# Second layer's attention: VectorE instead of ScalarE copies the mask of each odd key tile's second score bank into PSUM

## The chip, the cores and the metric

The kernel runs on one core of a Trainium2 chip. The metric is the device time of one execution in microseconds (us). TensorE does the matrix products, ScalarE (ACT) and VectorE (DVE) the elementwise work, GpSimd (POOL) some more of it, and SyncE (SP) issues DMA transfers. PSUM is the memory of eight banks that TensorE writes its products to; a bank holds 512 fp32 values in each of 128 partitions.

## What is computed

A small network of six blocks runs over x, 2 sequences of 256 rows with 256 features. Two of the blocks are cross attentions over a context of 4096 keys for each sequence. The change concerns the second one:

```
Q = query @ Wq.T + bq;  K = key @ Wk.T + bk;  V = value @ Wv.T + bv      # 16 heads of 16 features
energy = einsum('bhqd,bhkd->bhqk', Q, K) / sqrt(16)
energy = where(mask == 0, -1e20, energy)                                   # mask: 256 queries x 4096 keys
attention = softmax(energy, axis=-1)
x = x + einsum('bhqk,bhkd->bhqd', attention, V) ... @ Wo.T + bo
```

The first cross attention is the same without the mask, with a relative position bias. Between them lie a state-space block and a gated feed-forward block, behind them a time-mixing block and a quantized feed-forward block.

## The kernel before

**Steps.** Both attentions are done in 8 steps (g, b): g is one of 4 groups of four heads, b one of 2 sequences. The order is (0,0), (0,1), (1,0), ..., (3,1). A step goes twice over its keys.

**Units: the row maxima.** In the first pass there are 64 units (4 heads x 2 tiles of 128 queries x 8 chunks of 512 keys). TensorE multiplies (L477) into one of three PSUM banks, in turn; VectorE reads the bank, adds the mask and takes the maximum (L582, in the first attention L579 without mask). The semaphore at_seen counts read units, and TensorE writes unit u only when unit u - 3 has been read. When all 64 are read, VectorE makes the negated maxima of the step and splits them in three bf16 parts: five small instructions, L593 to L601, called the maxima below (`at_dve_top`). TensorE transposes these (L497, called rows) into one of the same three banks, and ScalarE writes them as three more rows of the queries (L609, two instructions). With them the scores come out with the maximum already subtracted.

**Score tiles: softmax and values.** In the second pass there are 32 key tiles i of 128 keys. Tile i uses PSUM banks 0 and 1 if i is even, 2 and 3 if it is odd, two heads to a bank. The first bank's mask is put there by a matmul with the identity (L511). The second bank's mask is copied there by ScalarE (L632) right after its exp of tile i - 2 (L628) has freed the banks, and TensorE waits for that copy (semaphore at_masked) before it adds the third and fourth head's scores (L520). Tiles 0 and 1 of a step have both masks from matmuls. After exp, TensorE multiplies with the values (L539) into bank 6, and ScalarE saves that bank at the end of a step (L617).

**How the passes mix.** TensorE's order is written out in `at_pe_step`: while it does the score tiles of step `cur` it does the units of step `nxt`. In pair j of key tiles (j = 0 to 15) it does scores 2j + 2, half of the pair's units, scores 2j + 3, the other half, then the values of tiles 2j and 2j + 1. PER_PAIR gives the units of each pair: 5, then 4 eleven times, 5, 2, 4, 4. From pair 13 on (OWN) the units are the first ten (LEAD) of the step `after` the next. So units 0 and 1 of that step come with scores 28 and 29, units 2 to 5 with scores 30 and 31, and then the rows of `nxt`; pair 15 does scores 0 and 1 of `nxt` with units 6 to 9. Each engine's queue is served strictly in the order written.

**Loops.** TensorE's loop runs over g for 3 passes of two steps, and group 3 is written out behind it. ScalarE's loop has 3 passes between written-out ends. VectorE's loop of the second attention (L699) has 4 passes of two steps, 406 instructions to a pass; in the first attention the step (0,1) stands ahead of the loop, and the loop has 3 passes.

Of the kernel before, what the change touches and what calls it, by code (L numbers as in the profile page):

```python
# [14 lines left out]
B, T, D = 2, 256, 256  # L15
# [8 lines left out]
NG = H // HG  # L24
NT = S // 128
# [18 lines left out]
PER_PAIR = (5, 4, 4, 4, 4, 4, 4, 4, 4, 4, 4, 4, 5, 2, 4, 4)  # L44
OWN = 13
LEAD = sum(PER_PAIR[OWN:])


def unit(u):

    q, r = divmod(u, UNITS // 4)
    hh, r = divmod(r, 4)
    tt, c2 = divmod(r, 2)
    return q, hh, tt, 2 * q + c2


def build(nc, A, out):
    ctx = ExitStack()
    with ctx:
# [5 lines left out]
        def sem(name):  # L65
            if name not in sems:
                sems[name] = ctx.enter_context(nc.semaphore(name))
            return sems[name]
# [40 lines left out]
        PS = ctx.enter_context(nc.psum_tensor("PS", [128, 8, 512], F32))  # L109
# [8 lines left out]
        def probs(i):  # L118
            return Pz[:, 1024 * (i % 4):1024 * (i % 4) + 1024]
# [47 lines left out]
        maskTs = Tz[:, 2 * S:4 * S].rearrange("p (i t) -> p i t", i=NT)  # L167
# [263 lines left out]
        def at_group(g, scale, more=0):  # L431

            return g[0] * scale + (g[1] * scale + more)

        def at_step(L, g, b, scale, more=0):

            return at_group(g, 2 * scale, (2 * NG * L + b) * scale + more)
# [21 lines left out]
        def ubank(b, u):  # L459

            return UBANK[(u + b) % 3]
# [39 lines left out]
        def at_pe_scores(e, L, g, b, i):  # L501
            if L == 0 and b == 0 and i == 0:
                e.wait_ge(sem("bias_cols"), at_group(g, 16, 16))
            if i == 0:
                e.wait_ge(sem("at_qrows"), at_step(L, g, b, 2, 2))
            e.wait_ge(sem("at_exp"), at_step(L, g, b, NT, i + 1))
            for hh in range(HG):
                bank = 2 * (i % 2) + hh // 2
                o = (hh % 2) * T
                if L == 1 and (hh == 0 or hh == 2 and i < 2):  # L510
                    e.matmul(PS[:, bank, :].rearrange("p (h t) -> p h t", h=2), identb[:, :],  # L511
                             maskTs[:, i:i + 1, :].broadcast_to([128, 2, T]), start=True, stop=False,
                             skip_group_check=True)
                elif L == 1 and hh == 2:


                    e.wait_ge(sem("at_masked"), at_step(0, g, b, NT - 2, i - 1))
                q = Qz[0:KROWS, bass.ds(at_group(g, 4 * R, hh * R + b * T), T)]
                bias = L == 0 and i < 3
                m = e.matmul(PS[:, bank, o:o + T], Kz[b][0:KROWS, hh, i * 128:i * 128 + 128], q,  # L520
                             start=(L == 0), stop=not bias, skip_group_check=True)
                if bias:

                    near = 128 if i == 2 else 0
                    for part in range(3):
                        c = 256 - 128 * i
                        m = e.matmul(PS[:, bank, o + near:o + T], flipb[:, :], bias_cols[:, hh * 3 + part, c + near:c + T],  # L527
                                     start=False, stop=(part == 2), skip_group_check=True)
            m.then_inc(sem("at_scores"), 1)
# [14 lines left out]
        def at_pe_units(e, L, j, part, nxt, after):  # L544
# [3 lines left out]
            if j < OWN:  # L548
                first, of = LEAD + sum(PER_PAIR[:j]), nxt
            else:  # L550
# [22 lines left out]
        def at_dve_unit(e, L, g, b, u, bank=None):  # L573
            q, hh, tt, c = unit(u)
            ps = PS[:, ubank(b, u) if bank is None else bank, :]
            e.wait_ge(sem("at_unit"), at_step(L, g, b, UNITS, u + 1))
            to = mx[:, 2 * hh + tt, c:c + 1]
            if L == 0:
                e.tensor_reduce(to, ps, AX.X, ALU.max).then_inc(sem("at_seen"), 1)  # L579
            else:  # L580
                e.sem_inc(sem("at_turn"), 1)
                e.tensor_tensor_reduce(junk[:, u % 3, :], ps, masks[:, tt, c * CH:c * CH + CH], 1.0, LOWEST,  # L582
                                       ALU.add, ALU.max, to).then_inc(sem("at_seen"), 1)

        def at_dve_units(e, L, g, b):
            for u in range(UNITS):
                at_dve_unit(e, L, g, b, u)
            at_dve_top(e, L, g, b)

        def at_dve_top(e, L, g, b):  # L590

            e.wait_ge(sem("at_seen"), at_step(L, g, b, UNITS, UNITS + 3))
            e.tensor_reduce(mneg[:, :], mx[:, :, :], AX.X, ALU.max, negate=True).then_inc(sem("at_top"), 1)  # L593
            e.wait_ge(sem("at_top"), at_step(L, g, b, 4, 1))
            e.tensor_copy(mparts[:, 0, :], mneg[:, :]).then_inc(sem("at_top"), 1)
            e.wait_ge(sem("at_top"), at_step(L, g, b, 4, 2))
            e.tensor_tensor(mres[:, :], mneg[:, :], mparts[:, 0, :], ALU.subtract).then_inc(sem("at_top"), 1)
            e.wait_ge(sem("at_top"), at_step(L, g, b, 4, 3))
            e.tensor_copy(mparts[:, 1, :], mres[:, :]).then_inc(sem("at_top"), 1)
            e.wait_ge(sem("at_top"), at_step(L, g, b, 4, 4))  # L600
            e.tensor_tensor(mparts[:, 2, :], mres[:, :], mparts[:, 1, :], ALU.subtract)\  # L601
                .then_inc(sem("at_mparts"), 1)

        def at_act_rows(e, L, g, b):
            e.wait_ge(sem("at_rows"), at_step(L, g, b, 1, 1))
            for k in range(2):
                p0 = 96 - 32 * k
                to = Qz[96:99, bass.ds(at_group(g, 4 * R, 2 * k * R), 2 * R)].rearrange("p (h r) -> p h r", h=2)
                e.activation(to[:, :, b * T:b * T + T], PS[p0:p0 + 3, rows_bank(b), :].rearrange("p (h t) -> p h t", h=2),  # L609
                             ACT.Identity).then_inc(sem("at_qrows"), 1)  # L610

        def at_act_out(e, L, g, b):

            e.wait_ge(sem("at_pv"), at_step(L, g, b, NT, NT + 4))
            if L == 1:
                e.wait_ge(sem("wq_done"), 1)
            e.activation(OTf[:, bass.ds(at_group(g, R, b * T), T)], PS[:, 6, 0:T], ACT.Identity)\  # L617
                .then_inc(sem("at_ocopied"), 1)

        def at_act_step(e, L, cur, nxt, before):  # L620
            for i in range(NT):
                e.wait_ge(sem("at_scores"), at_step(L, *cur, NT, i + 1))
                e.wait_ge(sem("at_pv"), at_step(L, *cur, NT, i + 1))
                if i == 2 and not before:
                    for s in range(2):
                        e.wait_ge(sem(f"kv_kstored{s}"), 96 * (NCH // 2 * (L + 1) + 1))
                        e.wait_ge(sem(f"kv_vstored{s}"), 16 * (NCH // 2 * (L + 1) + 1))
                e.activation(probs(i), PS[:, 2 * (i % 2):2 * (i % 2) + 2, :].rearrange("p a n -> p (a n)"), ACT.Exp)\  # L628
                    .then_inc(sem("at_exp"), 1)
                if L == 1 and i + 2 < NT:  # L630
                    e.wait_ge(sem("at_exp"), at_step(L, *cur, NT, i + 3))
                    e.activation(PS[:, 2 * (i % 2) + 1, :].rearrange("p (h t) -> p h t", h=2),  # L632
                                 maskTs[:, i + 2:i + 3, :].broadcast_to([128, 2, T]), ACT.Identity)\
                        .then_inc(sem("at_masked"), 1)
                if i == 0 and before:
                    at_act_out(e, L, *before)
                if i == NT // 2 and L == 1 and not nxt:
                    tm_act_decay(e)
                if i == NT - 2 and nxt:
                    at_act_rows(e, L, *nxt)  # L640
# [32 lines left out]
        def at_pe(e, L):  # L673
# [10 lines left out]
            for j in range(2):  # L684
                at_pe_scores(e, L, (0, 0), 0, j)
            for u in range(6, LEAD):
                at_pe_unit(e, L, (0, 0), 1, u, after_rows=3)
# [7 lines left out]
        def at_dve(e, L):  # L695
            if L == 0:
                at_dve_top(e, L, (0, 0), 0)
                at_dve_units(e, L, (0, 0), 1)
            with e.Fori(1 - L, NG) as g:  # L699
                at_dve_units(e, L, (g, 0), 0)  # L700
                at_dve_units(e, L, (g, 0), 1)

# [434 lines left out]
        def tm_act_decay(e):  # L1139
            e.wait_ge(sem("tm_exponents"), 1)  # L1140
            for t in (e1, e2, e1b, e2b):
                f = t.rearrange("p c t -> p (c t)")
                e.activation(f, f, ACT.Exp).then_inc(sem("tm_factors"), 1)
# [585 lines left out]
```

## Time and profile before

| | |
|---|---|
| median of 3 runs | 1521.8 us (1519.87 to 1525.97) |
| the profiled execution | 1515.61 us, its span 1513.8 us |
| second attention, score tiles | about 947 to 1418 us of the span |
| TensorE busy, matmuls (whole span) | 1333.2 us, 88% |
| VectorE busy | 986.1 us, 65% |
| ScalarE busy | 930.2 us, 61% |
| GpSimd busy | 203.2 us, 13% |
| mean granted TensorE clock | 0.927 of full speed |

Rows of the order of time give the start in us from the span's start, the duration in us, the engine (PE is a matmul, PEld TensorE's load of weights), the line, the operation, what it writes and reads, and how many alike were merged. A bracket at the end says how long the engine was idle before it and what ended that: an instruction of another engine, or "issue", when the profile shows nothing that was waited for. Busy shares hide which wait ends last, so they only say where to look.

### The profile page before, as it was taken

The page shows a single profiled execution, that of the slowest core. Times are in us where ns is not written, and L with a number is a line of the kernel's source. Part 1 is how long each engine was busy: PE and PEld are TensorE (multiplying, and loading weights), DVE is VectorE, ACT ScalarE, POOL GpSimd, SP SyncE. Part 2 cuts the span into 40 slices and gives each one's busy share as a digit, 9 for nine tenths or more (in the row PEclk, how much of TensorE's full clock was granted, in tenths as well). Part 3 has the DMA queues.
Part 4 walks back from the last instruction along what each step waited for, and adds up shares of the span by engine and source line. Part 5 has one row for each costly group of instructions (what it writes and reads, how often), then busy time and mean ns, then how long its engine had stood idle before and what let it go on. Part 6 is the DMA issues. An engine that isn't in the chain of part 4 may idle for free.

```text
span 1513.8 us, 32122 instructions
## 1 busy us (share of the span) xinstructions
PE 1333.2 (88%) x9431; PEld 700.1 (46%) x9432; DVE 986.1 (65%) x2169; ACT 930.2 (61%) x1179; POOL 203.2 (13%) x183
## 2 busy tenths in 40 slices
PE   7679899999999999779998639989999999998845
PEld 4346555545545555535554411444444444443523
DVE  4327777776776781259999439767667666773255
ACT  2227655555565568146666190879879788899404
POOL 1212200000000000019997040000000000000000
PEclk9889999999999999889999865999999999999975
DMA  4988774454454311106776864143434243400000
GB/s 157 207 265 269 224 175 100 85 118 108 78 117 111 74 29 59 63 1 207 254 253 219 222 102 104 35 82 68 77 59 86 59 87 59 85 2 22 1 0 14
DMA packets 108971, 164.09 MB, mean 108 GB/s; under 512 B 8528, under 2 KB 67408, under 8 KB 108320
## 3 DMA queue, kind: packets, MB, share of 16 engines
q1 hardware_dynamic: 107344, 160.78, 42.9%
q8 instruction: 92, 1.51, 0.4%
q10 hardware_dynamic: 1488, 1.42, 0.4%
q14 instruction: 47, 0.39, 0.1%
HBM read 116.96 MB, written 45.21 MB: 107 GB/s over the span
## 4 chain that ended last, share of the span: by engine, by line
PE 65%; DVE 12%; issue 11%; ACT 4%; SPq 3%; DMA 1%; DVEq 1%; POOL 1%; ACTq 0%; POOLq 0%
PE PS L539 15%; PE PS L477 15%; PE PS L520 14%; PE PS L511 4%; PE PS L255 3%; PE PS L264 2%; ACT Pz L628 2%; PE PS L484 2%; PE PS L527 2%; DVE Vz L996 1%; SPq L243 1%; DVE Kz L996 1%; DVE OT L1004 1%; DVE Pz L582 1%; PE PS L756 1%
## 5 line engine op out<-in xcount | busy, mean ns | idle before, releaser
L628 ACT ACTIVATE Pz<-PS 128x1024 f32<-128x1024 f32 x512 | 510.0, 1018 | 169.5 <-PE PS L520 148.2
L582 DVE CUSTOM_DVE_ANT_0 Pz<-PS,Tz 128x512 bf16<-128x512 f32 x512 | 323.0, 687 | 138.6 <-PE PS L477 123.9
L477 PE MATMUL PS<-Kz,Qz 96*128 96x512 bf16 x1024 | 364.7, 401 | 43.6 <-issue 21.9
L579 DVE TENSOR_REDUCE mx<-PS 128x1 f32<-128x512 f32 x512 | 320.7, 683 | 125.8 <-PE PS L484 70.2
L520 PE MATMUL PS<-Qz,Kz 99*128 (+1 forms) x2048 | 328.9, 275 | 6.9 <-ACT Pz L628 3.7
L539 PE MATMUL PS<-Pz,Vz 128*17 128x256 f32 x4096 | 277.4, 387 | 0.0
L520 PEld LDWEIGHTS PS<-Qz,Kz 99*128 99x128 bf16 x2048 | 188.7, 98 | 152.3 <-issue 54.7
L477 PEld LDWEIGHTS PS<-Kz,Qz 96*128 (+1 forms) x1024 | 100.5, 98 | 170.9 <-issue 105.7
L539 PEld LDWEIGHTS PS<-Pz,Vz 128*17 128x17 f32 x4096 | 101.3, 97 | 107.1 <-issue 42.8
L632 ACT ACTIVATE PS<-Tz 128x512 f32<-128x512 bf16 x240 | 144.3, 601 | 7.6
L511 PE MATMUL PS<-Tz,identb 128*128 128x512 bf16 x272 | 106.5, 392 | 15.5 <-ACT Pz L628 8.9
L333 POOL TENSOR_TENSOR Pz<-Pz 128x512 bf16<-128x512 f32 x64 | 79.9, 1257 | 148.5 <-ACT Pz L295 148.4
L373 POOL TENSOR_TENSOR rstd<-vare,nhalf 128x4 f32<-128x4 f32 x6 | 6.1, 1014 | 629.3 <-DVE vare L362 629.3
L255 PE MATMUL PS<-Pz,Vz 128*128 128x512 f32 x128 | 64.0, 624 | 23.4 <-DMA Pz<-in_ctxT 23.4
L511 PEld LDWEIGHTS PS<-Tz,identb 128*128 128x128 bf16 x272 | 26.3, 97 | 88.9 <-issue 50.4
L264 PE MATMUL PS<-Kz,Pz 128*128 128x256 f32 x256 | 62.2, 386 | 1.6 <-ACT Pz L290 0.3
L264 PE MATMUL PS<-Vz,Pz 128*128 128x256 f32 x256 | 60.8, 380 | 1.8 <-ACT Pz L290 1.8
L280 ACT ACTIVATE Pz<-PS 128x512 bf16<-128x512 f32 x32 | 19.1, 597 | 70.1 <-PE PS L255 44.4
L255 PE MATMUL PS<-Pz,Kz 128*128 128x512 f32 x128 | 62.1, 608 | 0.0
L609 ACT ACTIVATE Qz<-PS 3x512 f32 (+1 forms) x32 | 18.9, 589 | 67.9 <-PE PS L497 67.4
L264 PEld LDWEIGHTS PS<-Kz,Pz 128*128 128x128 f32 x256 | 47.7, 191 | 27.5 <-ACT Pz L290 13.9
L902 ACT ACTIVATE PS<-Kz,acoef 128x510 f32<-128x510 f32 x64 | 42.7, 685 | 28.7 <-DVE Kz L996 15.2
(223 smaller groups left out, 1257.4 us busy)
## 6 DMA issues: line engine op xcount, KB each, us to landing
k_parts<-Pz SPq DMA_DIRECT2D x192, 128.0 KB
Kz<-k_parts SPq DMA_DIRECT2D x64, 384.0 KB, 4.8
v_ones<-Pz SPq DMA_DIRECT2D x32, 544.0 KB, 5.0
Vz<-v_ones SPq DMA_DIRECT2D x64, 272.0 KB, 5.9
Pz<-in_ctxT SPq DMA_DIRECT2D x32, 512.0 KB, 5.7
Kz<-k_parts SPq DMA_DIRECT2D x64, 256.0 KB, 5.5
Kz<-k_parts SPq DMA_DIRECT2D x64, 128.0 KB, 5.8
Kz<-in_mask_pieces SPq DMA_DIRECT2D x16, 512.0 KB, 5.8
```

Of the source, the lines that this page charges most:

```text
L255: m = e.matmul(PS[:, 4 + half, :], wk[L][:, k, half * 128:half * 128 + 128], ctxb(s)[:, k, :], start=(k == 0), stop=(k == KC - 1))
L264: m = e.matmul(PS[:, 6, st * D:st * D + D], ctxb(s)[:, k, t * 128:t * 128 + 128], wv[L][:, k, :], start=(k == 0), stop=(k == KC - 1))
L333: e.tensor_tensor(kb(s, half, 2), kres(half), kb(s, half, 1), ALU.subtract)\
L477: m = e.matmul(PS[:, bank, :], Qz[0:ROWS, bass.ds(at_group(g, 4 * R, hh * R + b * T + tt * 128), 128)], Kz[b][0:ROWS, hh, c * CH:c * CH + ...
L511: e.matmul(PS[:, bank, :].rearrange("p (h t) -> p h t", h=2), identb[:, :], maskTs[:, i:i + 1, :].broadcast_to([128, 2, T]), start=True, s ...
L520: m = e.matmul(PS[:, bank, o:o + T], Kz[b][0:KROWS, hh, i * 128:i * 128 + 128], q, start=(L == 0), stop=not bias, skip_group_check=True)
L539: m = e.matmul(PS[32 * hh:32 * hh + VW, 6, 0:T], Vz[:, b, o:o + VW], probs(i)[:, hh * T:hh * T + T], start=(i == 0), stop=(i == NT - 1), s ...
L579: e.tensor_reduce(to, ps, AX.X, ALU.max).then_inc(sem("at_seen"), 1)
L582: e.tensor_tensor_reduce(junk[:, u % 3, :], ps, masks[:, tt, c * CH:c * CH + CH], 1.0, LOWEST, ALU.add, ALU.max, to).then_inc(sem("at_seen ...
L628: e.activation(probs(i), PS[:, 2 * (i % 2):2 * (i % 2) + 2, :].rearrange("p a n -> p (a n)"), ACT.Exp)\
L632: e.activation(PS[:, 2 * (i % 2) + 1, :].rearrange("p (h t) -> p h t", h=2), maskTs[:, i + 2:i + 3, :].broadcast_to([128, 2, T]), ACT.Iden ...
L902: e.activation(v3(abar[m_])[:, :, 1:T], v3(dt)[:, :, 1:T], ACT.Exp, scale=acoef[:, bass.ds(n * DC + m_, 1)]).then_inc(sem("ssm_abar"), 1)
```

## The change

In the seven steps that have a next step, the mask of odd tiles 3, 5, ..., 31 in the second bank (bank 3) is copied by VectorE. It waits for exp of tile i - 2 and signals a semaphore of its own, at_masked_odd. Even tiles, and all tiles of the last step, stay with ScalarE. The copies stand between VectorE's units of the next step: copy 2j + 3 ahead of the first unit of pair j for j = 0 to 12 (table MASK_AT), copies 29 and 31 behind unit 63 and ahead of the maxima. VectorE's first pass (g = 0) is written out ahead of the loop, which then has 3 passes.

```diff
+MASK_AT = tuple(LEAD + sum(PER_PAIR[:j]) for j in range(OWN))
...
-                    e.wait_ge(sem("at_masked"), at_step(0, g, b, NT - 2, i - 1))
+                    e.wait_ge(sem("at_masked_odd" if i % 2 else "at_masked"), at_step(0, g, b, NT // 2 - 1, i // 2))
...
-        def at_dve_units(e, L, g, b):
+        def at_dve_mask(e, g, b, i):
+
+            e.wait_ge(sem("at_exp"), at_step(1, g, b, NT, i + 1))
+            e.tensor_copy(PS[:, 3, :].rearrange("p (h t) -> p h t", h=2),
+                          maskTs[:, i:i + 1, :].broadcast_to([128, 2, T])).then_inc(sem("at_masked_odd"), 1)
+
+        def at_dve_units(e, L, g, b, before=None):
             for u in range(UNITS):
+                if before and u in MASK_AT:
+                    at_dve_mask(e, *before, 2 * MASK_AT.index(u) + 3)
                 at_dve_unit(e, L, g, b, u)
+            for i in range(2 * len(MASK_AT) + 3, NT, 2) if before else ():
+                at_dve_mask(e, *before, i)
             at_dve_top(e, L, g, b)
...
-                if L == 1 and i + 2 < NT:
+                if L == 1 and i + 2 < NT and (i % 2 == 0 or not nxt):
                     e.wait_ge(sem("at_exp"), at_step(L, *cur, NT, i + 3))
...
-                        .then_inc(sem("at_masked"), 1)
+                        .then_inc(sem("at_masked_odd" if i % 2 else "at_masked"), 1)
...
-            with e.Fori(1 - L, NG) as g:
-                at_dve_units(e, L, (g, 0), 0)
-                at_dve_units(e, L, (g, 0), 1)
+            if L == 0:
+                with e.Fori(1, NG) as g:
+                    at_dve_units(e, L, (g, 0), 0)
+                    at_dve_units(e, L, (g, 0), 1)
+            else:
+                at_dve_units(e, L, (0, 0), 0)
+                at_dve_units(e, L, (0, 0), 1, ((0, 0), 0))
+                with e.Fori(1, NG) as g:
+                    at_dve_units(e, L, (g, 0), 0, ((g, -1), 1))
+                    at_dve_units(e, L, (g, 0), 1, ((g, 0), 0))
```

VectorE, end of a pass of the loop, before (L582 is a unit, with the read of its maximum behind it; L593 to L601 are the maxima):

```order
L582 ISA Pz,mx<-PS,Tz 128x512 [waits at_unit]
L582 ISA mx 128x1
L592 ISA
L593 TENSOR_REDUCE mneg<-mx 128x8 [waits at_seen]
...
L601 TENSOR_TENSOR mparts<-mres,mparts 128x8 [waits at_top]
L699 REGISTER_ALU
L699 COMPARE_AND_BRANCH
```

The same place in the changed kernel (L583 is the unit, L589 the copy, L604 to L612 the maxima):

```order
L583 ISA Pz,mx<-PS,Tz 128x512 [waits at_unit]
L583 ISA mx 128x1
L588 ISA
L589 CAST PS<-Tz 128x512 [waits at_exp]
L588 ISA
L589 CAST PS<-Tz 128x512 [waits at_exp]
L603 ISA
L604 TENSOR_REDUCE mneg<-mx 128x8 [waits at_seen]
...
L612 TENSOR_TENSOR mparts<-mres,mparts 128x8 [waits at_top]
L717 REGISTER_ALU
L717 COMPARE_AND_BRANCH
```

Two copies, 29 and 31, now stand between unit 63 and the maxima, and a pass has 466 instructions.

VectorE, the place between step (0,1)'s maxima and step (1,0)'s units, in the changed kernel; before, the loop's COMPARE_AND_BRANCH shown above stood here:

```order
L589 CAST PS<-Tz 128x512 [waits at_exp] x2
L604 TENSOR_REDUCE mneg<-mx 128x8 [waits at_seen]
L606 CAST mparts<-mneg 128x8 [waits at_top]
L608 TENSOR_TENSOR mres<-mneg,mparts 128x8 [waits at_top]
L610 CAST mparts<-mres 128x8 [waits at_top]
L612 TENSOR_TENSOR mparts<-mres,mparts 128x8 [waits at_top]
L717 UNCONDITIONAL_BRANCH
L717 ISA
L583 ISA Pz,mx<-PS,Tz 128x512 [waits at_unit]
```

The loop is entered here instead of turned.

## Rows read from the trace of the kernel before

**Rows 1.** Busy time of each engine in one step's stretch.
```profile
core 0: us, PE busy (x) PEld busy (x) DVE busy (x) ACT busy (x) POOL busy (x), PEclk, DMA share, GB/s
1129.00:1189.00 60.00, 59.02 (x523) 28.72 (x513) 42.51 (x137) 53.36 (x69) 0.00 (x0) 0.98 0.38 73
```
**Rows 2.** Costliest groups by line: busy us, mean ns, idle before.
```profile
L632 ACT ACTIVATE PS<-Tz 128x512 f32<-128x512 bf16 x240 | 144.3, 601 | 7.6
```
**Rows 3.** Order of time, one inner pair of key tiles.
```profile
1172.04 1.01 ACT L628 ACTIVATE Pz<-PS 128x1024 f32<-128x1024 f32 x1
...
1174.13 0.69 DVE L582 CUSTOM_DVE_ANT_0 Pz<-PS,Tz 128x512 bf16<-128x512 f32 x1 [0.86 <-PE PS L477]
...
1174.75 0.69 DVE L582 CUSTOM_DVE_ANT_0 Pz<-PS,Tz 128x512 bf16<-128x512 f32 x1
...
1174.97 0.10 PEld L477 LDWEIGHTS PS<-Kz,Qz 96*128 x1 [0.33 <-issue]
...
1177.52 0.69 DVE L582 CUSTOM_DVE_ANT_0 Pz<-PS,Tz 128x512 bf16<-128x512 f32 x1 [0.86 <-PE PS L477]
```
**Rows 4.** Order of time, end of step (1,1), into (2,0).
```profile
1180.29 0.39 PE L511 MATMUL PS<-Tz,identb 128*128 128x512 bf16 x1
...
1180.70 0.22 DVE L593 TENSOR_REDUCE mneg<-mx 128x8 f32<-128x64 f32 x1
...
1181.82 0.69 DVE L582 CUSTOM_DVE_ANT_0 Pz<-PS,Tz 128x512 bf16<-128x512 f32 x1
...
1182.83 1.01 ACT L628 ACTIVATE Pz<-PS 128x1024 f32<-128x1024 f32 x1
...
1183.80 0.60 PE L477 MATMUL PS<-Kz,Qz 96*128 96x512 bf16 x2
...
1185.73 0.16 PEld L497 LDWEIGHTS PS<-identb,mparts 128*3 128x3 bf16 x6 [0.40 <-DVE mx L582]
...
1187.63 0.39 PE L511 MATMUL PS<-Tz,identb 128*128 128x512 bf16 x1 [0.20 <-ACT Qz L609]
```
**Rows 5.** Order of time, ends of (0,0) and (2,0), where VectorE's loop turns.
```profile
999.10 0.10 PEld L511 LDWEIGHTS PS<-Tz,identb 128*128 128x128 bf16 x1 [0.42 <-issue]
...
1011.26 0.10 PEld L511 LDWEIGHTS PS<-Tz,identb 128*128 128x128 bf16 x1 [0.83 <-ACT Pz L628]
...
1240.98 0.39 PE L511 MATMUL PS<-Tz,identb 128*128 128x512 bf16 x1
...
1247.07 0.69 DVE L582 CUSTOM_DVE_ANT_0 Pz<-PS,Tz 128x512 bf16<-128x512 f32 x1 [4.46 <-issue]
```
**Rows 6.** Order of time, first attention, VectorE enters its loop.
```profile
236.79 0.17 DVE L601 TENSOR_TENSOR mparts<-mres,mparts 128x8 bf16<-128x8 f32 x1
236.99 1.29 DVE L579 TENSOR_REDUCE mx<-PS 128x1 f32<-128x512 f32 x2
```
**Rows 7.** Order of time, start of step (2,1).
```profile
1257.50 1.02 ACT L628 ACTIVATE Pz<-PS 128x1024 f32<-128x1024 f32 x1
...
1258.22 0.69 DVE L582 CUSTOM_DVE_ANT_0 Pz<-PS,Tz 128x512 bf16<-128x512 f32 x1 [0.44 <-PE PS L477]
...
1259.66 0.56 PEld L477 LDWEIGHTS PS<-Kz,Qz 96*128 x3
```
**Rows 8.** Groups by line and shape, VectorE's copies.
```profile
L369 DVE COPY xnT<-PS 128x512 f32<-128x512 f32 x5 | 3.5, 691 | 7.1 <-PE PS L379 7.1
...
L405 DVE CAST Kz<-Kz 128x1024 bf16<-128x1024 f32 x1 | 0.7, 694 | 0.0
```
**Rows 9.** Order of time, TensorE's two loop turns.
```profile
1073.78 0.39 PE L511 MATMUL PS<-Tz,identb 128*128 128x512 bf16 x1 [2.62 <-issue]
...
1194.18 0.39 PE L511 MATMUL PS<-Tz,identb 128*128 128x512 bf16 x1 [3.18 <-issue]
...
1195.85 1.06 PE L520 MATMUL PS<-Qz,Kz 99*128 x4
```
**Rows 10.** Order of time, end of (3,0), into (3,1).
```profile
1360.43 1.01 ACT L628 ACTIVATE Pz<-PS 128x1024 f32<-128x1024 f32 x1
...
1362.44 0.10 PEld L497 LDWEIGHTS PS<-identb,mparts 128*3 128x3 bf16 x4 [0.21 <-issue]
```

## The prediction

> **What bounds the kernel now.** The table of stretches comes first: in the step from 1129 to 1189 us TensorE is busy 59.0 of 60 us, ScalarE 53.4 and VectorE 42.5 [rows 1]. ScalarE is nearly full and VectorE has room, which is what the change trades on, but neither is the bound: TensorE is. The mask copies that the change halves are 240 ScalarE instructions of 601 ns [rows 2].
>
> Second comes the order of time inside one pair of key tiles. A pair lasts 3.39 us (from the unit at 1174.13 to the one at 1177.52). VectorE sits idle 0.86 us ahead of its first unit. TensorE's own waits are two short ones named "issue"; the one of 0.33 ahead of the weights at 1174.97 is the pair's fourth unit, which waits until VectorE has read its first unit (a bank is reused every third unit). No wait inside the pair is for a mask [rows 3]. So in the inner pairs the change can take nothing off TensorE's path; it can only fail to fit.
>
> Third come the two ends of a step, where the handovers are serial: units done, five small VectorE instructions for the row maxima, TensorE rows, ScalarE rows, first scores of the next step. From the mask matmul of scores 28 (1180.29) to that of the next step's scores 0 (1187.63) it takes 7.34 us [rows 4]. Where VectorE's own loop turns in that place it takes 12.16 us (999.10 to 1011.26), since VectorE stands 4.46 us after the maxima before its next unit [rows 5]. These are the places that the change touches.
>
> **The change part by part.** Steps are called (g, b); seven of the eight have a next step, and in those the copies of tiles 3, 5, ..., 31 go to VectorE, 15 each, 105 in all.
>
> *Removed from ScalarE:* 105 x 0.60 = 63 us of copies. In an inner pair ScalarE's exp of the even tile waits for the scores and not for the copy before it, so its times stay; nothing is gained on TensorE's path. Taken at 0, covered by TensorE's own work. In the last step ScalarE keeps all copies: 0.
>
> *Added to VectorE: the price of one copy.* Before shows no VectorE copy from SBUF to PSUM. Nearest is the copy of the same size out of PSUM, 0.69 us; far off is a cast of 1024 elements between SBUF tensors, also 0.69, so 0.35 for 512 [rows 8]. I take 0.65, since consecutive VectorE instructions overlap a little (units of 0.69 start 0.62 apart, 1174.13 and 1174.75 [rows 3]), and keep 0.35 and 0.8 (0.69 without overlap and a tenth for the wait). Contention with GpSimd is out: it does nothing here [rows 1].
> The Trainium skill (VectorE: DVE Perf Modes, The perf-mode tier table) lets a copy with a PSUM operand reach at most twice the base rate. With that page's fixed 120 cycles for a PSUM source, used here as an estimate, that is (120 + 256) / 0.96 GHz = 0.39 us at double rate, and 0.66 us at base rate. By the double rate the sum below would be some 3 us smaller. No row of before decides it.
>
> *Inner pairs.* The copy for odd tile 2j+3 stands in front of the pair's first unit and waits for exp(2j+1). That exp ends at 1172.04 + 1.01 = 1173.05, VectorE is free at 1174.13 - 0.86 = 1173.27, the copy ends at 1173.92 and the unit can start at 1174.13 as before [rows 3]. It fits with 0.2 us to spare: 0.
>
> *End of a step.* Copies 29 and 31 stand after unit 63 and before the maxima. Copy 29 is harmless. Copy 31 waits for exp(29), which starts at 1182.83 and ends at 1183.84. Before, the maxima began at 1180.70 and the next unit, the first of the step after next, at 1181.82, so the block of maxima takes 1.12 us. Now: 1183.90 + 0.65 + 1.12 = 1185.67 for that unit, 3.85 us late; it ends at 1186.36. TensorE meets this at once: of the two units at 1183.80 the second is the fourth of its series and needs the first one read. It would go at 1184.02 and now goes at about 1186.5: 2.5 us of standing. Scores 31, two more units, the rows at 1185.73 and the next scores at 1187.63 are queued behind it in order, so all come 2.5 us later [rows 4]. Price per such end: +2.5.
>  - Into (1,0), (2,0), (3,0), where VectorE's loop doesn't turn: 3 x 2.5 = +7.5.
>  - Into (1,1) and (2,1), where it turns: before, the unit came 1247.07 - 1240.98 = 6.09 us after scores 28 [rows 5]. Now the maxima end 5.28 us after them (1185.67 - 0.10 - 1180.29), and the turn's 4.46 follows: 9.74. The turn does not overlap the new wait, because the branch stands behind both. 2 x 3.65 = +7.3.
>  - Into (0,1): the first pass is written out, so what was a turn is now the loop's entry. In the first layer's attention the loop is entered at the same point, and VectorE goes from the maxima (236.79) to the next unit (236.99) without a gap [rows 6]. So this end takes 7.34 + 2.5 = 9.84 instead of 12.16: -2.3.
>    The Trainium skill (Runtime: NRT & Kernel Launch, Instruction fetch mechanics) says that a taken branch stalls for a fetch only if its target lies outside the two blocks the sequencer holds. By it the entry, whose target follows directly, is free, and the turn of a body of over 400 instructions is not. Were any taken branch to pay, this term would be +2.2.
>  - Into (3,1): no unit follows the maxima; only the rows wait. exp(29) ends at 1361.44, copy and maxima end at 1363.25, and the rows go at some 1363.4 instead of 1362.44 [rows 10]: +1.0.
>
> *Start of a step.* Copy 3 waits for exp(1), which is late there because ScalarE first saves the last output: 1257.50 to 1258.52. VectorE's unit, before at 1258.22, now begins after the copy, at 1259.22, 1.0 us late. Of the three units at 1259.66 the third needs the second unit of the pair read: at 1259.22 + 2 x 0.62 + 0.2 = 1260.66, where it went at about 1260.1 [rows 7]. +0.6, then the pair's spare time takes it up. This holds for the first step and the starts into (0,1), (1,1), (2,1), (3,0): 5 x 0.6 = +3.0. Into (1,0) and (2,0) TensorE's own loop turns and stands 2.6 to 3.2 us [rows 9], in which exp(1) and the copy get done: 0.
>
> *Elsewhere* nothing changes; DMA issues wait for values matmuls and move with them.
>
> **Sum:** 7.5 + 7.3 - 2.3 + 1.0 + 3.0 = +16.5 us. The profiled execution took 1515.6, so its successor would take 1532.1. It lies 6.2 below the median of 1521.8, to which I carry the sum: **1538.3 us**, 1.1% slower. Bounds: with the copy at 0.35, twelve places of 0.3 less: +12.9; at 0.8: +18.3. If the entry stalls too: +4.5. And a long standstill lowers TensorE's clock: after 3.18 us the four score matmuls took 1.06 us, after 2.62 they did not slow at once [rows 9]; the new 2.5 us stands are just below, and if they count, about 1 us each at four ends. Together 12.9 to 27, that is 1535 to 1549, and 3 us either way for the spread of runs.
>
> **The rivals.**
> 1. *The copy doesn't fit the inner pair.* Spare is 0.2 us [rows 3]; a copy with its wait of over 0.85 would push every unit. For: it stands in front of a unit that TensorE awaits. Against: 0.69 in the nearest row. At 1.0 it costs 0.15 in 13 pairs of 7 steps, 14 us more: 1552.
> 2. *ScalarE sets the pair after all, and the kernel gets faster.* It is busy 53.4 of 60 us [rows 1]. If the pair's stall of TensorE went back to late evacuation by ScalarE, the pair would fall from 3.39 to 3.17; 0.22 in 15 pairs of 7 steps is 23 us, and exp(29) would come half a microsecond earlier at each end: 1538 - 27 = 1511. It wins over the forecast's losses from 0.23 us saved in each pair. Against: the stalled unit waits for VectorE's reading, which starts right when TensorE delivers.
> 3. *Nothing.* The delays at the ends vanish in waits that are there anyway (ScalarE's two row copies, TensorE's turn): 1522. Against: at the ends I find these waits behind the delay in one chain, not beside it.
>
> **How the numbers follow.** Forecast 0.80, rival 1 0.07, rival 2 0.04, rival 3 0.09. Half a per cent, 7.6 us, is about what a measurement of this kernel can tell from no change. Slower: forecast and rival 1, less a little for a forecast whose losses come out half as large, 0.86; same: rival 3 and that little, 0.10; faster 0.04. The range reaches down past the forecast's own 1532 to losses of a third the size, and up to rival 1: 1526 to 1553.
>
> **What would show it.** In the new profile: 105 VectorE casts of about 0.65 us and 135 ScalarE copies; inner pairs still 3.39 us; at the ends a TensorE wait of some 2.5 us on VectorE ahead of a unit where before there was none, and one of some 7 us, where before 3 to 3.5, at the two turns; three VectorE "issue" waits of 4.5 reduced to two. I am wrong if pairs change length, if the wait at the ends is missing, or if the maxima begin before exp(29) has ended.

## The result, and the profile after

| | before | after |
|---|---|---|
| median of 4 runs | 1520.84 us (1517.95 to 1525.97) | 1537.45 us (1535.49 to 1539.46) |
| the profiled execution | 1515.61, span 1513.8 | 1535.49, span 1533.4 |
| VectorE busy | 986.1 | 1050.0 |
| ScalarE busy | 930.2 | 867.5 |
| mean granted TensorE clock | 0.927 | 0.923 |

The ratio is 1.0109 (95%: 1.0075 to 1.0144): slower by 1.1%, where 1538.3 us was forecast. ScalarE got its 63 us off and VectorE took 64 on. By medians the loss is 16.6 us, between the spans of the two profiled executions 19.6.

The costliest groups of the changed kernel by line (busy us, mean ns | idle before); the second and fourth answer to [rows 2]:

```profile
L583 DVE CUSTOM_DVE_ANT_0 Pz<-PS,Tz 128x512 bf16<-128x512 f32 x512 | 322.9, 687 | 72.7 <-PE PS L478 65.7
L589 DVE CAST PS<-Tz 128x512 f32<-128x512 bf16 x105 | 72.5, 690 | 23.7 <-ACT Pz L639 23.7
...
L643 ACT ACTIVATE PS<-Tz 128x512 f32<-128x512 bf16 x135 | 81.2, 602 | 4.3
```

There are 105 copies on VectorE and 135 left on ScalarE. VectorE stood 23.7 us in all ahead of its copies, waiting for an exp.

The order of time in one inner pair of the changed kernel, which answers to [rows 3]:

```profile
1151.23 1.01 ACT L639 ACTIVATE Pz<-PS 128x1024 f32<-128x1024 f32 x1
...
1152.38 0.69 DVE L589 CAST PS<-Tz 128x512 f32<-128x512 bf16 x1
...
1153.32 0.69 DVE L583 CUSTOM_DVE_ANT_0 Pz<-PS,Tz 128x512 bf16<-128x512 f32 x1 [0.25 <-PE PS L478]
...
1154.16 0.10 PEld L478 LDWEIGHTS PS<-Kz,Qz 96*128 x1 [0.33 <-issue]
...
1156.71 0.69 DVE L583 CUSTOM_DVE_ANT_0 Pz<-PS,Tz 128x512 bf16<-128x512 f32 x1 [0.25 <-PE PS L478]
```

The copy fits. VectorE's idle time ahead of the pair's first unit shrank from 0.86 to 0.25 us and is still idle time, so the unit waits for TensorE's scores as it did. The pair lasts 3.39 us (1153.32 to 1156.71), and the wait of 0.33 ahead of the fourth unit's weights is unchanged.

The end of step (1,1), into (2,0), in the order of time; it answers to [rows 4]:

```profile
1186.63 0.39 PE L512 MATMUL PS<-Tz,identb 128*128 128x512 bf16 x1
...
1189.16 1.01 ACT L639 ACTIVATE Pz<-PS 128x1024 f32<-128x1024 f32 x1
...
1190.20 0.69 DVE L589 CAST PS<-Tz 128x512 f32<-128x512 bf16 x1 [2.60 <-ACT Pz L639]
...
1190.81 0.21 DVE L604 TENSOR_REDUCE mneg<-mx 128x8 f32<-128x64 f32 x1
...
1191.92 0.69 DVE L583 CUSTOM_DVE_ANT_0 Pz<-PS,Tz 128x512 bf16<-128x512 f32 x1
...
1192.77 0.39 PE L478 MATMUL PS<-Kz,Qz 96*128 96x512 bf16 x1 [2.23 <-DVE mx L583]
...
1193.21 0.60 PE L521 MATMUL PS<-Qz,Kz 99*128 x4
...
1194.50 0.16 PEld L498 LDWEIGHTS PS<-identb,mparts 128*3 128x3 bf16 x6 [0.36 <-DVE mx L583]
...
1196.40 0.39 PE L512 MATMUL PS<-Tz,identb 128*128 128x512 bf16 x1 [0.20 <-ACT Qz L620]
```

This is where most of the loss arises. exp(29) runs from 1189.16 to 1190.17; copy 31 waits 2.60 us for it at the head of VectorE's queue. The maxima, which needed nothing of it, start at 1190.81, 4.18 us after scores 28's mask matmul instead of 0.41; the next unit comes 5.29 after it instead of 1.53. TensorE stands 2.23 us at the fourth unit of the new series. From scores 28 to the next scores 0 it is 9.77 us instead of 7.34.

The end of (1,0), where VectorE's loop turns; it answers to [rows 5]:

```profile
1125.28 0.69 DVE L589 CAST PS<-Tz 128x512 f32<-128x512 bf16 x1 [2.60 <-ACT Pz L639]
...
1130.15 0.69 DVE L583 CUSTOM_DVE_ANT_0 Pz<-PS,Tz 128x512 bf16<-128x512 f32 x1 [3.24 <-issue]
...
1131.00 0.61 PE L478 MATMUL PS<-Kz,Qz 96*128 96x512 bf16 x1 [5.41 <-DVE mx L583]
```

The turn follows the wait and does not overlap it, but it takes 3.24 us here and at the end of (2,0), where before had 4.54 and 4.46. TensorE stands 5.41 us in both places, where before had 3.11 and 3.05.

The end of (0,0), where the loop was turned before and is entered now:

```profile
1002.83 0.69 DVE L583 CUSTOM_DVE_ANT_0 Pz<-PS,Tz 128x512 bf16<-128x512 f32 x1 [0.19 <-issue]
...
1003.68 0.61 PE L478 MATMUL PS<-Kz,Qz 96*128 96x512 bf16 x1 [2.28 <-DVE mx L583]
...
1004.51 1.06 PE L521 MATMUL PS<-Qz,Kz 99*128 x4
```

The entry costs 0.19 us. After the stand of 2.28 us TensorE's granted clock is down, 0.50 of full speed from 1004 to 1007 us: the unit of 512 columns takes 0.61 instead of 0.39, the four score matmuls 1.06 instead of the 0.60 of (1,1) above.

The start of step (0,1), where copy 3 waits for exp(1); the bracket on the score matmul shows that here TensorE is held by a mask:

```profile
1013.54 0.69 DVE L589 CAST PS<-Tz 128x512 f32<-128x512 bf16 x1 [1.06 <-ACT Pz L639]
...
1014.38 0.41 PE L521 MATMUL PS<-Qz,Kz 99*128 x2 [0.21 <-DVE PS L589]
...
1015.59 0.39 PE L478 MATMUL PS<-Kz,Qz 96*128 96x512 bf16 x1 [0.23 <-DVE mx L583]
```

All of it, laid out by step. TensorE works in order, so the times between its mask matmuls divide the attention: a step's start (scores 0 to 4), its eleven inner pairs (scores 4 to 26; 36.3 to 37.4 us), the pair from scores 26 to 28, and its end (scores 28 to the next step's scores 0), in us from the traces:

| step | start before | after | end before | after | change of both |
|---|---|---|---|---|---|
| (0,0) | 9.45 | 9.12 | 12.15 | 10.83 | -1.65 |
| (0,1) | 7.83 | 8.59 | 7.33 | 10.82 | +4.25 |
| (1,0) | 10.31 | 11.26 | 11.85 | 15.07 | +4.17 |
| (1,1) | 7.77 | 8.53 | 7.34 | 9.77 | +3.19 |
| (2,0) | 11.96 | 12.46 | 12.70 | 14.34 | +2.14 |
| (2,1) | 7.79 | 8.82 | 7.34 | 10.79 | +4.48 |
| (3,0) | 7.54 | 8.13 | 6.40 | 7.36 | +1.55 |

The ends give +13.9, the starts +4.3, the inner pairs together 0.1, the pair from 26 to 28 nothing (4.0 us, or 3.9 in (3,0), on both sides), and the last step's inner pairs 0.55: 18.8 of the 19.6 us between the spans.

### The profile page after: what moved, and what is told of

Read it like the earlier page. It is cut to its first block, busy times and chain, and to the rows that moved or that the text cites. A ratio compares the mean times of both kernels' runs of the same rounds, so it can differ in the third digit from the quotient of the medians.

```text
span 1533.4 us, 31983 instructions
## 1 busy us (share of the span) xinstructions
PE 1342.8 (88%) x9432; PEld 703.2 (46%) x9432; DVE 1050.0 (68%) x2274; ACT 867.5 (57%) x1074; POOL 203.4 (13%) x183
## 4 chain that ended last, share of the span: by engine, by line
PE 60%; DVE 14%; issue 14%; ACT 5%; SPq 3%; POOL 2%; DVEq 1%; DMA 1%; ACTq 0%; POOLq 0%
PE PS L540 15%; PE PS L478 14%; PE PS L521 14%; PE PS L512 4%; ACT Pz L639 3%; PE PS L256 2%; PE PS L485 2%; PE PS L528 2%; DVE Pz L583 2%; PE PS L265 2%; DVE Vz L1014 1%; DVE OT L1022 1%; SPq L244 1%; DVE Kz L1014 1%; PE PS L774 1%
## 5 line engine op out<-in xcount | busy, mean ns | idle before, releaser
L583 DVE CUSTOM_DVE_ANT_0 Pz<-PS,Tz 128x512 bf16<-128x512 f32 x512 | 322.9, 687 | 72.7 <-PE PS L478 65.7
L589 DVE CAST PS<-Tz 128x512 f32<-128x512 bf16 x105 | 72.5, 690 | 23.7 <-ACT Pz L639 23.7
L643 ACT ACTIVATE PS<-Tz 128x512 f32<-128x512 bf16 x135 | 81.2, 602 | 4.3
L265 PEld LDWEIGHTS PS<-Kz,Pz 128*128 128x128 f32 x256 | 47.7, 191 | 27.6 <-ACT Pz L291 13.9
```

What stands on the lines that cost most here:

```text
L265: m = e.matmul(PS[:, 6, st * D:st * D + D], ctxb(s)[:, k, t * 128:t * 128 + 128], wv[L][:, k, :], start=(k == 0), stop=(k == KC - 1))
L589: e.tensor_copy(PS[:, 3, :].rearrange("p (h t) -> p h t", h=2), maskTs[:, i:i + 1, :].broadcast_to([128, 2, T])).then_inc(sem("at_masked_o ...
```

## The experiments

Theory A is the forecast's: the loss is copy 31's wait ahead of the maxima, a little is copy 3's wait at the start, the copies of the inner pairs are free, and writing out VectorE's first pass gives some of it back. Its rivals here: the copies cost as such (VectorE's load), or the turn and its new place make the difference. Every ratio is to the kernel before, run on the same chip beside them: its median was 1520.84 us beside the change, 1519.25 with experiments 1 to 4, 1521.69 with 5 to 8, 1519.08 with 9 and 10. The last column is, of one trace each, the time from scores 0 of (0,0) to scores 0 of (3,1), less the 415.95 us of before; it leaves out the rest of the kernel, which varies by some us of its own (the stretch begins between 947.1 and 954.6 us in the twelve traces, though nothing ahead of it was changed). A trace is one execution, from 6.1 us above its kernel's median (2) to 3.5 below it (1); so the medians carry the totals, and the stretches say where the time lies.

| kernel | median us | ratio (95%) | stretch |
|---|---|---|---|
| the change | 1537.45 | 1.0109 (1.0075 to 1.0144) | +18.2 |
| 1: copies 3 to 27 | 1515.45 | 0.9978 (0.9961 to 0.9995) | -5.0 |
| 2: copy 31 alone | 1536.25 | 1.0109 (1.0078 to 1.0140) | +19.8 |
| 3: written-out pass alone | 1516.12 | 0.9981 (0.9965 to 0.9997) | -2.7 |
| 4: all copies, 31 later | 1519.65 | 0.9990 (0.9970 to 1.0011) | +0.7 |
| 5: copies 5 to 27 | 1509.02 | 0.9929 (0.9904 to 0.9955) | -7.8 |
| 6: these, each twice | 1546.96 | 1.0174 (1.0143 to 1.0205) | +30.2 |
| 7: before, VectorE without a loop | 1502.34 | 0.9869 (0.9845 to 0.9894) | -14.3 |
| 8: before, VectorE and TensorE without | 1490.22 | 0.9787 (0.9760 to 0.9815) | -30.3 |
| 9: the change, both without | 1514.50 | 0.9971 (0.9959 to 0.9983) | -3.5 |
| 10: copies 5 to 27, both without | 1488.26 | 0.9803 (0.9791 to 0.9816) | -28.0 |

**1. Copies 29 and 31 back to ScalarE.** The changed kernel, with a table of what VectorE copies; experiments 2 and 5 differ in that table alone.

```diff
+BY_DVE = range(3, 28, 2)
...
-                if before and u in MASK_AT:
+                if before and u in MASK_AT and 2 * MASK_AT.index(u) + 3 in BY_DVE:
...
-                at_dve_mask(e, *before, i)
+                if i in BY_DVE:
+                    at_dve_mask(e, *before, i)
...
-                if L == 1 and i + 2 < NT and (i % 2 == 0 or not nxt):
+                if L == 1 and i + 2 < NT and (i % 2 == 0 or not nxt or i + 2 not in BY_DVE):
```

> The changed kernel with copies 29 and 31 given back to ScalarE: VectorE keeps 13 of 15 copies per step (91 in all). Theory A (the cost is that copy 31 holds the maxima back until exp(29) has ended): the ends of the steps are free again, 7.3 us where VectorE's loop does not turn and at its entry, 10.5 to 12 us at the two turns; the starts still cost 0.5 to 1 us each. Against the kernel before: about +4 for the starts, -4.8 for the end of step (0,0), -1 to -3 for the turns: -1 to -4 us, 1517 to 1521. Theory B (each copy on VectorE costs alike, wherever it stands): 91/105 of the loss stays, +14 us, 1535.

1515.45 us, below the 1517 of the lower end, but 3.8 less than before measured beside it, which is inside the -1 to -4. With 91 of the 105 copies still on VectorE the loss is gone. The ends without a turn are back at 7.34 us, that of (0,0) at 7.23.

**2. Copy 31 alone on VectorE.**

```diff
-BY_DVE = range(3, 28, 2)
+BY_DVE = (31,)
```

> The changed kernel with only copy 31 on VectorE, one per step (7 in all), all others on ScalarE. Theory A: the ends cost all that they cost in the changed kernel (9.8 to 10.8 us without a turn, 14 to 15 with one), the starts nothing: the changed kernel less 4 us, about +12 to +13 against before, 1533 to 1534. Theory B (each copy costs alike): 7/105 of the loss, +1 us. Theory C (the written-out first pass makes the loss, not the copies): the same +16 as the changed kernel.

1536.25 us, the same ratio as the whole change: seven copies make a loss as large as 105 do. The time alone would also fit theory C, the written-out pass; the waits below and experiment 3 decide against it. That the totals agree so closely is in part chance: by the stretch the ends cost more here than in the changed kernel (+16.9 against +13.9; the end of (1,1) takes 12.16 us, with the granted clock down in it) and the starts less (+2.0 against +4.3). What stands is that copy 31 alone is enough for the loss at the ends. TensorE's and VectorE's waits of this kernel in the second attention (us in total, times, longest):

```profile
PE PS L479 <- DVE mx L584: 22.7, 15, 5.4
...
DVE PS L590 <- ACT Pz L641: 22.2, 7, 3.2
```

TensorE stands 22.7 us at units that wait for VectorE. The same wait in the changed kernel:

```profile
PE PS L478 <- DVE mx L583: 23.0, 19, 5.4
```

And in the kernel before:

```profile
PE PS L477 <- DVE mx L582: 11.5, 12, 3.4
```

So 11.5 us of it are new with the whole change, and 11.2 with copy 31 alone.

**3. The written-out pass alone.** The kernel before, with VectorE's first pass of the second attention ahead of its loop.

```diff
-            with e.Fori(1 - L, NG) as g:
+            if L == 1:
+                at_dve_units(e, L, (0, 0), 0)
+                at_dve_units(e, L, (0, 0), 1)
+            with e.Fori(1, NG) as g:
```

> The kernel before with VectorE's first pass written out ahead of the loop and nothing else changed; all copies on ScalarE. Theory A: only the end of step (0,0) changes, from 12.2 to 7.3 us, since the entry of the loop does not stall: -4.8 us, 1516. Theory C (a loop's entry stalls like its turn, or the longer code costs): no gain, or a loss.

1516.12 us by the median, 3.1 less than before. The end of (0,0) fell from 12.15 to 7.23 us; what is missing from 4.8 in this trace is at the other two turns, whose ends came out 1.2 and 0.3 us longer, and in inner pairs (+1.3). So the written-out pass does not cost; it gives a little.

**4. All copies on VectorE, copy 31 behind the maxima.** It follows the first two units of the next series.

```diff
             for u in range(UNITS):
+                if last and u == 2:
+                    at_dve_mask(e, *last, NT - 1)
...
-            for i in range(2 * len(MASK_AT) + 3, NT, 2) if before else ():
+            for i in range(2 * len(MASK_AT) + 3, NT - 1, 2) if before else ():
```

> The changed kernel with all 105 copies on VectorE, but copy 31 moved behind the maxima and the first two units of the next series (in the last of them behind the maxima alone). Theory A: the ends fall from 9.8-10.8 to 7.3-7.7 us, the turns lose 2.5 us, the starts stay: +0 to +2 us against before, 1520 to 1523. Theory B (the number of copies on VectorE costs): no change against the changed kernel, +16.

1519.65 us: the loss is gone with all 105 copies in place, so it was the order and not the number of copies. The order of time at the end of (0,1):

```profile
1063.82 0.21 DVE L606 TENSOR_REDUCE mneg<-mx 128x8 f32<-128x64 f32 x1
...
1064.93 0.69 DVE L583 CUSTOM_DVE_ANT_0 Pz<-PS,Tz 128x512 bf16<-128x512 f32 x1
...
1066.50 0.69 DVE L589 CAST PS<-Tz 128x512 f32<-128x512 bf16 x1 [0.26 <-ACT Pz L641]
```

The maxima start before exp(29) has ended, the copy waits 0.26 us instead of 2.60, and this end takes 7.43 us. It doesn't beat before: the starts together are 5.3 us longer, most at (0,1) with 9.49 against 7.83, where part of it is TensorE's granted clock, 0.50 of full speed from 1018.7 us on.

**5. Only the inner copies, 5 to 27.**

```diff
-BY_DVE = range(3, 28, 2)
+BY_DVE = range(5, 28, 2)
```

> The changed kernel with copies 5 to 27 alone on VectorE (12 per step, 84 in all); 3, 29 and 31 on ScalarE. Theory A: these copies cost nothing at all, and the starts are free too. What is left is the written-out first pass: the same time as with that pass alone, about -5 us by the step's ends against before, 1514 to 1516, and 2 to 3 us less than with copy 3 on VectorE. Theory B (each copy on VectorE costs): 84/105 of the loss, +13 us.

1509.02 us, 5 below what was expected. The starts that copy 3 had lengthened are shorter than in experiment 1, 7.82 us against 8.35 at (0,1) and 7.54 against 8.19 at (3,0), though (2,1) with 8.19 against 8.24 hardly is. Beyond that the two ends with a turn took 10.79 and 9.84 us, where before has 11.85 and 12.70; the turns themselves show 3.74 and 3.92 us of "issue". Of the 5.5 us by which this trace's span is below that of experiment 1, 2.8 lie in the stretch, 2.2 ahead of it and 0.5 behind it, where nothing was changed.

Experiment 3 is this kernel without the 84 copies on VectorE, and 5 is faster than it: 0.9929 against 0.9981, with intervals that do not meet. So with the loops in place the inner copies did bring about half a per cent. The traces put it at the two ends with a turn, 20.6 us together against 26.0, with only 1.1 us in the inner pairs. Why the turns became cheaper is open, and without loops nothing of it is left (experiment 10).

**6. The inner copies twice.** As 5, but each of the 84 copies is done two times, the second waiting for the first.

```diff
             e.tensor_copy(PS[:, 3, :].rearrange("p (h t) -> p h t", h=2),
+                          maskTs[:, i:i + 1, :].broadcast_to([128, 2, T])).then_inc(sem("at_twice"), 1)
+            e.wait_ge(sem("at_twice"), at_step(0, g, b, 12, (i - 3) // 2))
+            e.tensor_copy(PS[:, 3, :].rearrange("p (h t) -> p h t", h=2),
                           maskTs[:, i:i + 1, :].broadcast_to([128, 2, T])).then_inc(sem("at_masked_odd"), 1)
```

> The kernel with copies 5 to 27 on VectorE, each done twice, the second waiting for the first. Theory A: an inner pair has 0.86 us of idle VectorE ahead of its first unit, which one copy of 0.62 to 0.69 fits and two (1.3 with the wait) do not: pairs with copies lengthen by 0.4 to 0.5 us, from 3.39 to about 3.8, 12 pairs in 7 steps, +34 to +42 us against one copy each, 1550 to 1557. Rival (ScalarE or the scores set the pair): pairs stay at 3.39 and the time stays.

1546.96 us, 37.9 above experiment 5 by medians and 38.0 by the stretch. The order of time in one pair:

```profile
1022.77 0.69 DVE L590 CAST PS<-Tz 128x512 f32<-128x512 bf16 x1
...
1023.49 0.69 DVE L593 CAST PS<-Tz 128x512 f32<-128x512 bf16 x1
...
1024.10 0.68 DVE L584 CUSTOM_DVE_ANT_0 Pz<-PS,Tz 128x512 bf16<-128x512 f32 x1
```

VectorE has no idle time left: each instruction follows the last by 0.61 to 0.72 us. The added copy takes 0.72 and the pairs take 3.81 us instead of 3.39, so 0.42 of it is paid and 0.30 was spare. The pairs account for 34 of the 38 us; the two ends with a turn give 3.7 more (12.32 and 12.00 us, with turns of 4.99 and 4.77). So the first copy was free and the second is paid for, as a spare of 0.2 to 0.3 us has it, and it bounds rival 1: that rival was near.

**7. The kernel before, VectorE's passes all written out.** **8.** TensorE's too. **9.** The changed kernel with both written out. **10.** As 8, with copies 5 to 27 on VectorE.

```diff
-            with e.Fori(1 - L, NG) as g:
-                at_dve_units(e, L, (g, 0), 0)
-                at_dve_units(e, L, (g, 0), 1)
...
+                for g in range(NG):
+                    at_dve_units(e, L, (0, g), 0)
+                    at_dve_units(e, L, (0, g), 1)
...
+                for g in range(NG - 1):
+                    at_pe_step(e, L, ((0, g), 0), ((0, g), 1), ((0, g + 1), 0))
+                    at_pe_step(e, L, ((0, g), 1), ((0, g + 1), 0), ((0, g + 1), 1))
```

> The kernel before with all four of VectorE's passes of the second attention written out, no loop; all copies on ScalarE. Theory A (the turn's stall is a matter of the branch back): all seven ends take 7.3 us (the last 6.4), 4.9 + 4.5 + 5.4 less: about -14 us, 1505. Rival (each new pass pays a fetch however it is reached): no change.

> As the kernel before, with VectorE's passes and TensorE's three passes of the second attention written out. Theory A: besides VectorE's 14 us, the starts of (1,0) and (2,0), 10.3 and 12.0 us with TensorE's turn, fall to 7.8: another -6 to -7, about 1498. Rival: TensorE's longer code costs fetches of its own and nothing more is gained.

> The changed kernel, all 105 copies on VectorE, with VectorE's and TensorE's passes of the second attention written out. Theory A: without any turn each of six ends pays for copy 31, 2.5 us or 3.5 where TensorE's clock falls after the stand, the last 1.0; each of seven starts 0.6 to 1.0: +21 to +27 us over the kernel of e8 (1490), 1511 to 1517, about as fast as the kernel before. Rival (the loss needs the turns, copy 31 alone is covered): below 1500.

> The kernel of e8 (no turns) with copies 5 to 27 on VectorE. Theory A (TensorE and its handover with VectorE set the pair): pairs stay at 3.30 us, 1490, no difference to e8. Rival (ScalarE, busy 3.2 of 3.3 us there, now sets the pair): pairs fall to 3.2 or below, 0.1 us in 80 pairs, 1482 or less.

Experiment 7's stretch is 14.3 us shorter, as expected (the median 19): the three turns were worth that. Experiment 8 gained 30 where 21 was expected. Against experiment 7 its two starts at which TensorE's loop had turned fell by 8.4 us together (11.52 and 11.79 to 7.47 each), and its pairs got shorter, which was not forecast:

```profile
1144.46 0.69 DVE L582 CUSTOM_DVE_ANT_0 Pz<-PS,Tz 128x512 bf16<-128x512 f32 x1 [0.77 <-PE PS L477]
...
1145.21 0.10 PEld L477 LDWEIGHTS PS<-Kz,Qz 96*128 96x128 bf16 x1 [0.24 <-DVE mx L582]
...
1147.76 0.69 DVE L582 CUSTOM_DVE_ANT_0 Pz<-PS,Tz 128x512 bf16<-128x512 f32 x1 [0.77 <-PE PS L477]
```

A pair takes 3.30 us instead of 3.39. The fourth unit's weights now wait 0.24 us and the trace names VectorE, where inside the loop it said "issue" and 0.33. Before's step (3,0), which TensorE runs outside its loop, shows the same: 36.31 us for eleven pairs against 37.31 to 37.39 in the six steps ahead of it.

Experiment 9 is 24.3 us above 8 by medians (26.8 by the stretch): without a turn of either loop the change costs what theory A says, and more than with the loops, because the written-out first pass no longer gives anything back. Its ends take 9.7 to 11.0 us, the last 7.36, against 7.25 to 7.35 and 6.41 in 8. Its starts show the price of copy 3 most cleanly: 8.12 us against 7.47 at (1,0), (2,0) and (3,0). TensorE's waits for VectorE ahead of a unit in experiment 9:

```profile
PE PS L478 <- DVE mx L583: 15.7, 21, 2.1
```

And in experiment 10:

```profile
PE PS L479 <- DVE mx L584: 2.2, 10, 0.2
```

Experiment 10 ends where 8 does (1488.26 and 1490.22 us measured beside different runs of before; ratios 0.9803 and 0.9787, whose intervals overlap). The pairs stay at 3.30 us: 84 copies taken off ScalarE bring nothing here, and cost nothing. Both kernels are some 2% faster than the kernel before and 3% faster than the changed one, by leaving the loops out.

## Why the prediction was right

It gave 1538.3 us, a range of 1526 to 1553, and slower with 0.86; 1537.45 was measured, by the mechanism that it named. The agreement is closer than the terms deserve. Each against the traces:

| term | forecast | measured |
|---|---|---|
| inner pairs, seven steps | 0 | +0.1 |
| ends into (1,0), (2,0), (3,0) | +7.5 | +3.49, +2.43, +3.45 = +9.4 |
| ends into (1,1), (2,1) | +7.3 | +3.22, +1.64 = +4.9 |
| end into (0,1) | -2.3 | -1.3 |
| end into (3,1) | +1.0 | +1.0 |
| starts | +3.0 | +4.3 |
| last step's pairs, elsewhere | 0 | +1.3 |
| sum (terms rounded) | +16.5 | +19.6 |

- *The chain at the end of a step* was read right. The maxima block began 4.18 us after scores 28 and the unit came 5.29 after (forecast 5.38). Where the clock held, at (1,1), the end grew by 2.43 against the 2.5 forecast. Experiments 2 and 4 show the cause from both sides: copy 31 alone is enough, and moving it alone takes the loss away.
- *The clock* was the term left out. That stands of 2.5 us might lower it stood only in the bounds, with about 1 us at each of four ends; it did at (0,0), (0,1) and (2,1), with 1 us each, and not at (1,1). The table of stretches shows the two levels (columns as in [rows 1]; PEclk is 1.00 at 2.4 GHz, and 0.83 a mean with a part at 1.2 GHz):

```profile
1120.00:1140.00 20.00, 14.36 (x116) 6.54 (x115) 9.79 (x32) 8.66 (x11) 0.00 (x0) 0.83 0.25 47
1180.00:1200.00 20.00, 17.05 (x155) 8.35 (x152) 14.56 (x46) 12.60 (x16) 0.00 (x0) 1.00 0.29 55
```

  The first stretch has the stand of 5.41 us in it, the second that of 2.23.
- *The turn* was the step that failed: "the turn's 4.46 follows". It took 3.24, so VectorE's unit came 8.45 us after scores 28 instead of 9.74. That is 1.3 us less at each of two ends. At (1,0) the clock then took 0.9 back: in before it was down there for only the last part of the end, from 1127.5 us on, with the change from before the unit at 1131.00 to the end's last matmul. At (2,0) it was down before and after, but with the change more of that time fell into the stand, so the end grew by 0.7 less. Before's low stretch at (1,0):

```profile
1127.50:1130.80 3.30, 3.30 (x32) 1.49 (x34) 1.85 (x6) 1.61 (x3) 0.00 (x0) 0.50 0.01 2
```

  The announced TensorE wait of some 7 us was 5.41.
- *The entry* was free. The Trainium skill (Runtime: NRT & Kernel Launch, Instruction fetch mechanics) had it so, since its target follows directly; the trace agrees with 0.19 us in place of 4.86. The 406 and 466 instructions to a pass, counted ahead of the result, leave out a semaphore increment for each of its 128 units, which the traces record: a pass has 534 in before and 594 in the change. By the same page of the Trainium skill a branch stalls when its target lies outside two blocks of 256 instructions, 512 in all. The traces agree: these passes are longer and their turns took 3.2 to 4.9 us, while the first attention's loop has 278 instructions to a pass and its turns took 0.39 and 0.37 us.
- *The copy's price* was set at 0.65 and is 0.690 us, 0.61 from one start to the next where it doesn't wait. The double rate of the Trainium skill (VectorE: DVE Perf Modes, The perf-mode tier table) is an upper bound, and the estimate of 0.39 us by it is not what this copy from SBUF into PSUM does; the estimate of 0.66 by the same page's base rate is near. The nearest row of before [rows 8] was the better guide.
- *The starts.* The term of 0.6 us for each of five starts was right in size. Experiment 9 against 8 gives 0.65 at (1,0), (2,0) and (3,0), where no loop turns and the granted clock holds in both; experiment 5 against 1 shows at (0,1) and (3,0) that it is copy 3. In the change the starts of (0,1), (1,1), (2,1) and (3,0) grew by 0.6 to 1.0 and that of the first step by nothing. The place where TensorE stands is another than the forecast's: the rows of (0,1) show its scores waiting 0.21 us for the mask, and the unit 0.23 behind that. Into (1,0) and (2,0), where TensorE's turn was thought to cover the copy, +0.95 and +0.50 were measured, but whether copy 3 makes them isn't shown: with copy 3 on ScalarE these two starts took 10.3 to 12.1 and 10.5 to 12.7 us in before and experiments 2, 3, 5 and 7.
- *Rivals.* 1 (the copy doesn't fit) fell: pairs of 3.39. 2 (ScalarE sets the pair) fell: in the changed kernel ScalarE is 63 us lighter and no pair is shorter, and experiment 10 shows it again without loops. (Its 0.23 us a pair is what would make the kernel half a per cent faster; 16.5 us over 105 pairs are made up for by 0.16.) 3 (nothing) fell: the delay is in one chain with what follows it.

The sum was 3.1 us short against its own execution, and the median of after lies 2.0 above its profiled execution where that of before lay 6.2 above in the three runs that the forecast had: the two nearly cancel, which is luck. The miss in the terms is the honest measure, 1 to 2.4 us in five of the seven.

What stays open: why the turn takes 3.2 us in some kernels and 4.5 in others. It was 3.0 to 3.3 in the change and in experiments 2 and 4, 3.7 to 3.9 in 5, 4.2 to 4.9 in 1, 3 and before, and 4.8 to 5.0 in 6. Among these bodies the length doesn't order them (534 instructions before and in 3, 538 in 2, 582 in 5, 586 in 1, 594 in the change and 4, 630 in 6). In the change and in 2 VectorE had stood 2.6 to 3.2 us for an exp just ahead of the maxima and the branch, in 4 it hadn't. No run was made for it.

## What to carry to other kernels

When work is handed to an engine with time to spare, ask what stands behind it in that engine's queue, and place the instruction that waits longest behind those that need no wait: here seven copies alone cost 1.1%, and moving them behind five small instructions and two units took it back. A lighter ScalarE shortened no pair here, since none waits for its masks, and spare time in a pair is worth measuring by doubling the load. Loop turns were a larger prize than the balance of the engines: written-out passes gave 2%.

## What the runs showed that I had not expected

- A loop on TensorE costs inside the body too. The pair's fourth unit goes 0.09 us later than in written-out code (0.33 "issue" against 0.24 for VectorE; pairs of 3.39 and 3.30 us). In step (3,0) of before and in experiment 8 the wait that is left is put down to VectorE; so the "issue" that the forecast read as the bank's reuse was that only in part. In the loop the addresses come from a register; that this is the reason isn't shown.
- Whether TensorE's granted clock falls at a stand isn't told by the stand's length alone. In the change it held at 1.00 behind the stand of 2.23 us at (1,1) and was down to 0.50 behind those of 2.25 to 2.28 at (0,0), (0,1) and (2,1). Experiment 9 has stands of 2.07 us at five ends; the clock held at (0,1) and (1,0) and fell at the other three. Its units behind the stands of (0,1) and (1,1), and the clock after each:

```profile
1069.94 0.39 PE L478 MATMUL PS<-Kz,Qz 96*128 96x512 bf16 x1 [2.07 <-DVE mx L583]
...
1187.01 0.39 PE L478 MATMUL PS<-Kz,Qz 96*128 96x512 bf16 x1 [2.07 <-DVE mx L583]
```

```profile
1070.00:1074.00 4.00, 3.57 (x42) 1.78 (x43) 2.94 (x10) 1.53 (x3) 0.00 (x0) 1.00 0.01 2
1189.00:1191.00 2.00, 2.00 (x26) 1.16 (x29) 1.01 (x4) 1.26 (x3) 0.00 (x0) 0.50 0.00 0
```

- Two VectorE instructions in a row overlap by 0.07 to 0.08 us (0.69 long, 0.61 apart) whether they are copies or units, but the second of two copies where it waits for the first starts 0.72 after it.
